# Attention in a six-layer stack: probabilities turned in 32x32 blocks on VectorE, weighed by 32 keys on four row groups, and a new order of work

## The reference

```
q, k, v = split(x @ Wqkv)                 # 3 x 1024 columns
q = l2norm(q) per head;  k = l2norm(k) per head
q = q*cos + rotate_half(q)*sin            # position tables, scaled
k = k*cos' + rotate_half(k)*sin'
for each block of 32 queries: sim = q @ k.T over the 64 keys of its own block and the one before
sim = where(mask, -max, sim);  attn = softmax(sim)
out = attn @ v;  x = out @ Wo             # 1024 -> 128, added to x
x = x + W2 @ (lin * gelu(gate)),  lin, gate = W1 @ layernorm(x)
```

## Time and profile before

| | us |
|---|---|
| median of 3 runs | 3809.59 |
| lowest and highest run | 3805.08, 3809.89 |
| span of the profiled execution | 3803.9 |
| stack0: first projection to last MLP product | 105.9 to 1734.7 |
| mixer | between the stacks |
| stack1: last MLP product | 3797.6 |

### The profile page before, as it was taken

One profiled execution on the slowest core, in us unless ns is written; L12 is line 12 of the kernel. 1 busy time (PEld: TensorE's weight loads), 2 busy tenths in 40 slices (PEclk: granted clock), 3 DMA queues, 4 the chain that ended last, 5 costly groups with the idle time before them and its releaser, 6 DMA issues. The chain is left out here.

```text
span 3803.9 us, 157044 instructions
## 1 busy us (share of the span) xinstructions
PE 3594.4 (94%) x61680; PEld 2336.5 (61%) x61680; DVE 3264.6 (86%) x11515; ACT 2374.7 (62%) x4331; POOL 2752.8 (72%) x2632
## 2 busy tenths in 40 slices
PE   6799999999999999997699689999999999999998
PEld 4466666666666666662466456666666666666665
DVE  6898888888888889865799798889898888889885
ACT  2567667666766767663422257667676766767665
POOL 1788888878888888852144288888887888888883
PEclk9899999999999999998799699999999999999999
DMA  1232323323322332220000132233233232332222
GB/s 46 77 85 71 81 73 78 87 67 74 85 73 69 85 75 66 66 65 16 0 1 6 29 81 72 74 87 78 71 80 76 71 81 74 83 78 68 66 69 57
DMA packets 170286, 250.95 MB, mean 66 GB/s; under 512 B 36544, under 2 KB 67264, under 8 KB 169408
## 3 DMA queue, kind: packets, MB, share of 16 engines
q1 hardware_dynamic: 169536, 240.72, 25.4%
HBM read 38.21 MB, written 1.05 MB: 10 GB/s over the span
## 5 line engine op out<-in xcount | busy, mean ns | idle before, releaser
L592 PE MATMUL stack_work<-stack_w_qkv,stack_xs 128*128 128x512 f32 x2304 | 1148.0, 604 | 34.4 <-ACT stack_sq L883 17.8
L1244 POOL TENSOR_TENSOR stack_roped<-stack_rot_c,stack_rot_s 128x512 f32<-128x512 f32 x768 | 984.6, 1304 | 148.5 <-DVE stack_rot_s L1052 148.2
L1254 POOL TENSOR_TENSOR stack_roped<-stack_roped,stack_rnorm 128x512 f32<-128x512 f32 x768 | 794.6, 1045 | 188.7 <-DVE stack_rnorm L1084 188.7
L883 ACT ACTIVATE stack_sq<-stack_work 128x512 f32<-128x512 f32 x768 | 443.3, 594 | 485.6 <-DVE stack_rot_s L1052 485.1
L1050 DVE TENSOR_TENSOR stack_rot_c<-stack_work,rot_tables 128x512 f32<-128x512 f32 x768 | 526.8, 686 | 130.4 <-PE stack_work L592 112.9
L592 PEld LDWEIGHTS stack_work<-stack_w_qkv,stack_xs 128*128 128x128 f32 x2304 | 400.5, 191 | 384.4 <-issue 323.9
L1270 POOL TENSOR_TENSOR stack_s_m<-stack_s_m,stack_inv 128x512 f32<-128x512 f32 x384 | 400.8, 1044 | 276.4 <-DVE stack_inv L1113 276.1
L1052 DVE TENSOR_TENSOR stack_rot_s<-stack_work,rot_tables 128x512 f32<-128x512 f32 x768 | 521.6, 679 | 0.0
L1061 DVE TENSOR_REDUCE stack_ssq<-stack_sq 128x8 f32<-128x512 f32 x768 | 496.7, 667 | 6.0 <-issue 4.4
L641 PEld LDWEIGHTS stack_bank_o<-stack_p_t,stack_v_w 64*64 64x64 f32 x24576 | 394.5, 135 | 171.9 <-issue 147.4
L600 PE MATMUL stack_work<-ident,stack_roped 128*128 128x128 f32 x3072 | 452.2, 280 | 8.3 <-issue 5.8
(11 more groups left out here) (257 smaller groups left out, 5269.0 us busy)
## 6 DMA issues: line engine op xcount, KB each, us to landing
stack_v_w<-stack_v_nat SPq DMA_DIRECT2D x1152, 128.0 KB
stack_v_w<-stack_v_nat SPq DMA_DIRECT2D x768, 64.0 KB
stack_w_qkv<-table_ffn_qkv SPq DMA_DIRECT2D x192, 96.0 KB, 2.3
stack_w_o<-table_ffn_wo SPq DMA_DIRECT2D x12, 512.0 KB, 4.2
stack_w<-table_ffn_w SPq DMA_DIRECT2D x12, 384.0 KB, 3.3
stack_w<-table_ffn_w SPq DMA_DIRECT2D x12, 192.0 KB, 3.1
x_outer<-L_attn_a_X SPq DMA_DIRECT2D x4, 256.0 KB, 6.9
ret_xpos<-table_xpos SPq DMA_DIRECT2D x1, 1024.0 KB, 6.2
```

What stands on the lines that cost most here:

```text
L592: pe.matmul(bank[:, :], xs[:, T, :], w_qkv[:, g.half, col:col + 512], start=True, stop=True).then_inc(done["proj_" + c], 1)
L883: act.activation(sq[:, i % 2, :], work[(BANK["p_" + c][T] + g.row) % 4][:, :], ACT.Square).then_inc(done["squared_" + c], 1)
L1244: pool.tensor_tensor(roped[:, i, T % 2, :], rot_c[:, i % 2, :], rot_s[:, i % 2, :], ALU.add).then_inc(done["roped_" + c], 1)
L1254: pool.tensor_tensor(r, r, rnorm[:, T % 2, i, :].unsqueeze(2).broadcast_to([P, 8, HD]), ALU.mult).then_inc(done["united_" + c], 1)
```

## The change: what it does

- VectorE turns the probabilities, in 32x32 blocks in SBUF (a new step `turn_probs` on VectorE, two instructions of 128x512 per tile). TensorE's `turn_probs` and ScalarE's `probs_out` go.
- `weigh` is one step with 128 products per tile: 32 rows (keys) each, 64 columns, 32 moving columns, on 4 row groups by 2 column groups. For each block of queries the product with the keys before and that with its own keys are added in PSUM. Each row group writes its own bank. The own keys' values are read in place from `v_nat` (now four tiles deep); only the values 32 positions back are moved, with two transfers per tile in place of ten.
- The four banks `quad` hold the scores (banks 0 and 1) and the weighed heads (all four). `weigh` waits until the masks of the scores before are through, `scores` until `heads_out` has copied the heads. `heads_out` is one copy of 128x1024.
- q is not normed by POOL: its inverse norm is the scale of each mask pass, a value per partition. `unit` is left for k0 and k1 only.
- POOL's `stage` goes; projections read `xst` directly.
- `scores` is one step with all 64 products; it waits for all four chunks.
- All engines get a new order, written out for each T, with other lags (first projection at lag 3, weighing at 8, `project_out` at 9 or 8), a new bank table, and four more slots at the end of a stack.

The core of the diff:

```diff
-        v_nat = sb("v_nat", [P, 2, 2, 8, HD])
-        v_w = sb("v_w", [P, 2, 4, 8, HD])
+        v_nat = sb("v_nat", [P, 4, 2, 8, HD])
+        v_prev = sb("v_prev", [P, 2, 2, 8, HD])
...
-        p_t = sb("p_t", [P, 2, 4, P])
+        p_t = sb("p_t", [P, 2, 2, PAIRS, 2, WINDOW])
...
-        bank_s = [ps("bank_s0"), ps("bank_s1")]
-        bank_o = ctx.enter_context(nc.psum_tensor(shared["tag"] + "bank_o", [P, 2, 512], F32))
+        quad = ctx.enter_context(nc.psum_tensor(shared["tag"] + "quad", [P, 4, 512], F32))
...
-            run_slots(16 * (DEPTH - 1), 4 * (DEPTH - 1), DEPTH - 1, 1, 16 + 12)
+            run_slots(16 * (DEPTH - 1), 4 * (DEPTH - 1), DEPTH - 1, 1, 16 + 16)
...
-                for gp in range(2):
-                    half = 64 * gp
-                    sp.dma_start(v_w[half + 32:half + 64, b, 0, :, :], v_nat[0:32, b, gp, :, :]).then_inc(v_in[b], 16)
-                    sp.dma_start(v_w[half:half + 32, b, 0, :, :], v_nat[96:P, 1 - b, gp, :, :]).then_inc(v_in[b], 16)
-                    for n4 in range(1, 4):
-                        sp.dma_start(v_w[half:half + 64, b, n4, :, :], v_nat[32 * (n4 - 1):32 * (n4 + 1), b, gp, :, :]
-                                     ).then_inc(v_in[b], 16)
+                sp.dma_start(v_prev[WINDOW:P, b, :, :, :], v_nat[0:P - WINDOW, n % 4, :, :, :]).then_inc(v_in[b], 16)
+                sp.dma_start(v_prev[0:WINDOW, b, :, :, :], v_nat[P - WINDOW:P, (n - 1) % 4, :, :, :]).then_inc(v_in[b], 16)
...
-            def weigh(t, T, g, j):
...
-                for half in range(2):
-                    for n in range(4):
-                        for odd in range(2):
-                            for gp in range(2):
-                                m, at = 2 * half + odd, P * half + WINDOW * n
-                                last = pe.matmul(bank_o[HD * odd:HD * (odd + 1), gp, at:at + WINDOW],
-                                                 v_w[64 * gp:64 * gp + 64, T % 2, n, 2 * m + j, :],
-                                                 p_t[64 * gp:64 * gp + 64, j, m, WINDOW * n:WINDOW * (n + 1)],
-                                                 start=True, stop=True)
+            def weigh(t, T, g):
...
+                for j in range(2):
+                    for gp in range(2):
+                        for half in range(2):
+                            at = WINDOW * (4 * j + 2 * gp + half)
+                            for own in range(2):
+                                values = v_nat[:, T, gp, :, :] if own else v_prev[:, T % 2, gp, :, :]
+                                for n in range(4):
+                                    rows = slice(WINDOW * n, WINDOW * (n + 1))
+                                    for odd in range(2):
+                                        m = 2 * half + odd
+                                        last = pe.matmul(quad[HD * odd:HD * (odd + 1), n, at:at + WINDOW],
+                                                         values[rows, 2 * m + j, :], p_t[rows, T % 2, j, 2 * m + gp, own, :],
+                                                         start=not own, stop=bool(own))
+                last.then_inc(done["weighed"], 1)
...
+                act.copy(o_t[:, T % 2, :, :].rearrange("p i (n q) -> p n i q", n=4),
+                         quad[:, :, 0:PAIRS * WINDOW].rearrange("p n (i q) -> p n i q", q=WINDOW)
+                         ).then_inc(done["ot_set"], 1)
...
             def mask_max(t, T, g, j):
...
+                wait(dve, "unit_set", t)
+                apart(dve, t)
                 wait(dve, "scored", t)
-                wait(dve, f"pe_pt{j}", t - 2)
...
-                    last = dve.tensor_tensor_reduce(s_m[:, T % 2, j, hp, :], bank_s[j][:, 64 * hp:64 * hp + 64],
-                                                    mask[:, first:first + 2 * WINDOW], 1.0, LOWEST, ALU.add, ALU.max,
-                                                    smax[:, T % 2, j, hp:hp + 1])
+                    i, h = CHUNKS.index(f"q{hp // 4}"), 2 * (hp % 4) + j
+                    last = dve.tensor_tensor_reduce(s_m[:, T % 2, j, hp, :], quad[:, j, 64 * hp:64 * hp + 64],
+                                                    mask[:, first:first + 2 * WINDOW], rnorm[:, T % 2, i, h:h + 1],
+                                                    LOWEST, ALU.add, ALU.max, smax[:, T % 2, j, hp:hp + 1])
...
+            def turn_probs(t, T, g, j):
+                if not live(t):
+                    return
+                wait(dve, f"prob{j}", t)
+                wait(dve, "weighed", t - 2)
+                dve.transpose(p_t[:, T % 2, j, :, :, :].rearrange("p h f q -> p (h f q)"),
+                              s_m[:, T % 2, j, :, :].rearrange("p h k -> p (h k)")).then_inc(done[f"turned_p{j}"], 1)
```

More of the change, by code:

```diff
@@ L412, in ffn_stack @@
             "xn_nat", "x_turned", "x_back", "pe_back", "x_added"))
[L413 removed]
+        early = [quad[:, n, :] for n in range(4)]
         def natural(s):
@@ L583, in _, with project, turn @@
         def _(pe):
-            def project(t, T, g, c, bank):
+            def project(t, T, g, c):
                 if not live(t):
                     return
[L587 to L590, removed]
+                if c == FIRST_IN and T == 0:
+                    wait_x(pe, g.number - BATCH)
+                    apart(pe, t)
+                    pe.wait_ge(qkv_in, (g.layer + (layer0 + 1)) * 256)
                 col = 512 * PARTS[c]
-                pe.matmul(bank[:, :], xs[:, T, :], w_qkv[:, g.half, col:col + 512], start=True, stop=True
-                          ).then_inc(done["proj_" + c], 1)
-            def turn(t, T, g, c, bank):
+                pe.matmul(work[(BANK["p_" + c][T] + g.row) % 4][:, :], xst[:, g.row, P * T:P * (T + 1)],
+                          w_qkv[:, g.half, col:col + 512], start=True, stop=True).then_inc(done["proj_" + c], 1)
+            def turn(t, T, g, c):
                 if not live(t):
                     return
-                wait(pe, "united_" + c, t)
+                wait(pe, ("roped_" if c[0] == "q" else "united_") + c, t)
+                bank = work[(BANK["t_" + c][T] + g.row) % 4]
                 for n in range(4):
@@ L602, in turn, with scores @@
                 last.then_inc(done["turned_" + c], 1)
-            def scores(t, T, g, part):
+            def scores(t, T, g):
                 if not live(t):
                     return
-                wait(pe, f"kept_k{part}", t)
-                wait(pe, f"kept_q{part}", t)
-                apart(pe, t)
-                for hp in range(4 * part, 4 * part + 4):
+                for c in CHUNKS:
+                    wait(pe, f"kept_{c}", t)
+                    apart(pe, t)
+                for hp in range(PAIRS):
                     for j in range(2):
@@ L645, in weigh @@
-                last.then_inc(done[f"weighed{j}"], 1)
-            def project_out(t, T, g, bank):
-                if not live(t):
-                    return
-                wait(pe, "ot_set0", t)
-                wait(pe, "ot_set1", t)
+                wait(pe, "ot_set", t)
                 if T == 0:
                     pe.wait_ge(wo_in, (g.layer + (layer0 + 1)) * 16)
+                bank = work[(BANK["wo"][T] + g.row) % 4]
                 for n in range(PAIRS):
@@ L661, in center, with variance @@
                 wait(pe, "mid_set", 4 * g.number + 3)
-                pe.matmul(bank[:, :], center_m[:, :], mshift[:, g.pair, 0:SEQ], start=True, stop=True
+                pe.matmul(work[(BANK["ct"] + g.row) % 4][:, :], center_m[:, :], mshift[:, g.pair, 0:SEQ], start=True, stop=True
                           ).then_inc(done["pe_center"], 1)
-            def variance(g, bank):
+            def variance(g):
                 if not live_group(g):
@@ L668, in variance, with up @@
                 wait_group(pe, "center_sq", g)
-                pe.matmul(bank[:, :], mean_m[:, :], c_sq[:, :], start=True, stop=True).then_inc(done["pe_var"], 1)
-            def up(g, kind, k, bank):
+                pe.matmul(work[(BANK["va"] + g.row) % 4][:, :], mean_m[:, :], c_sq[:, :], start=True, stop=True
+                          ).then_inc(done["pe_var"], 1)
+            def up(g, kind, k):
                 if not live_group(g):
@@ L914, in values_out @@
                 wait(act, f"proj_v{gp}", t)
-                if live(t - 1):
-                    act.wait_ge(v_in[(T - 1) % 2], (2 * g.number + (tile0 // 2 + (T - 1) // 2 + 1)) * 160)
-                act.copy(v_nat[:, T % 2, gp, :, :],
+                wait(act, "weighed", t - 3)
+                act.copy(v_nat[:, T, gp, :, :],
                          work[(BANK[f"p_v{gp}"][T] + g.row) % 4][:, :].rearrange("p (h d) -> p h d", d=HD)
@@ L1229, in _ @@
         def _(pool):
-            def stage(t, T, g):
-                if not live(t):
-                    return
-                wait_x(pool, g.number - BATCH)
-                wait(pool, "proj_" + LAST_IN, t - 4)
-                apart(pool, t)
```

(1 more changed line is left out.)

694 lines of the change are left out of this document (394 added, 300 removed).

## The result

The changed kernel takes **4524.07 us** (median of 4 runs, 4511.60 to 4529.44), the kernel before 3807.34 (4 runs, 3804.12 to 3809.89). The ratio is 1.188, 95% interval 1.1861 to 1.1898. The forecast was 3835 and its range ended at 3970. The likeliest case had "slower" as the larger part of its chance, and slower it is, but by 717 us where 25 were forecast, and for a reason that no case had. The profiled execution has a span of 4509.7 us.

What follows compares the result with a forecast made beforehand. TensorE bounded the kernel before; the bound was to move to VectorE, 16.4 plus 0.15 of waits, 16.55 against 16.46 us per tile: +17 over 192 tiles, +12 at the ends, from 3809.6 to 3839, rounded to 3835; range 3680 to 3970.

Steps and rivals of the forecast that it cites:

- The likeliest case: Whole kernel: TensorE relieved by about 1 us, VectorE takes 2 us more and sets the pace; 3790 to 3900, chance 0.40.
- part (3) of TensorE: Weighing: 256 passes of 32 keys at 8.3 ns plus 0.1 for the pause, against 1.84 us now, +0.38 per tile.
- Transposes gone from TensorE (-0.93): TensorE: the eight transposes of the probabilities, two blocks, go; -0.93 us per tile.
- entries (-0.42): TensorE: scores and weighing one block each instead of two, so two fewer tiled blocks to enter and leave; -0.42 us per tile.
- Ends of the stacks (+12): First projection one slot later and last MLP product two: about +6 us per stack, +12.
- VectorE (16.4): VectorE per tile: 14.4 us, plus 1.26 for block transposes and 0.96 for mask-pass scale, less 0.2: 16.4 us.
- Rival C of the prediction: VectorE: a block transpose costs twice a pass, 1.2 us; VectorE 17.5, 4040 us, slower; chance 0.10.
- Rival A: VectorE: mask-pass scale costs nothing, or the norm's steps wait much less; VectorE 15.4, 3678 us, faster; chance 0.34.
- Rival B: TensorE: weighing passes stay at 14.4 ns on eight tiles; TensorE 16.9, slot 17.1, 3945 us, slower; chance 0.16.
- The ring of shared banks: Weighing, copy, scores and masks chained by shared banks set the slot; would need over 16 us, counted about 8; no chance.

Runs made afterwards that it cites:

- own_only: The changed kernel with the products with the keys before left out of weighing, 128 passes instead of 256, so another output; 3848.24 us.
- own_const: own_only with a constant 1.0 as the scale of the mask pass, so the query norm is left out too; 3689.25 us.
- split2: The changed kernel with weighing issued in two parts of 128 passes, other products between them, and slight shifts in order; 4128.56 us.
- scores_burst: The kernel before with the second half of the scores issued four times over, output unchanged; 4718.45 us.
- split4: The changed kernel with weighing issued in four parts of 64 passes and the scores in two parts; 4168.18 us.
- split2_qpool: split2 with a constant in the mask pass and POOL multiplying by the query norm instead; 4046.94 us.
- weigh_twice: The kernel before with every weighing product issued twice, output unchanged; 4181.83 us.

## Why the prediction was wrong

**The step that failed** is part (3) of TensorE, "256 x 8.3 = 2.12 us, plus 0.1". It was mis-sized in two ways. The first is the rate: 8.3 ns came from a stretch of 0.1 us, while the same rows have 64 passes in 0.65 us, 10.2 ns. Weighing runs near that at full clock (x132 in 1.27 us), and at 12.2 ns over the layer, its share of the lower clock included. The second is larger: the sum took for granted that a long burst goes on as a short one begins. It doesn't: 2.04 us per tile of standing still in weighing, 0.34 in the scores, and behind these the lower clock, with about 1.5 us more in the full-size products. With the rate that makes 5.0 us, and TensorE, forecast at 15.3, sets a slot of 20.3. So the bound did not move to VectorE, and that the change is slower, as the forecast had it, was luck: it had VectorE as the reason. Twice the passes, issued as one step, are what put 512 instructions in a row, and the one step I had booked as part of a gain of 0.42.

**Transposes gone from TensorE (-0.93), entries (-0.42).** own_only bears the rest of the sum out in part. With half of weighing's passes off, the forecast sum is 14.2 us a tile; TensorE is busy 15.0. The transposes' 0.93 went whole. Scores and weighing together fell from 3.72 to 2.92, about what fewer and faster passes were to give (0.78). But turns and projections took 0.34 more than before, and nothing of the 0.42 for entries can be seen; no run isolates it.

**Ends of the stacks (+12).** From a stack's first projection to its first scores it takes 32.5 us where it took 23.7, and from the last tile's scores to the last MLP product 53 in both kernels: about +18 for both stacks, where 12 were forecast.

**VectorE (16.4)** was right: 16.3 busy in the changed kernel, 16.5 as a bound in own_only. Behind a block transpose the next instruction starts after 0.627 us (own_only; 0.63 was taken, and the row below has its duration), and the mask passes start 0.205 us apart (0.20). Rival C of the prediction (1.2 us a transpose) is out. The Trainium skill, VectorE: DVE Perf Modes, The three transpose paths, has 311 ns for 128x128 in bf16; grown with the elements, the prediction's estimate of 1.24 us, it is twice the measured time.

```profile
L1121 DVE STREAM_TRANSPOSE stack_p_t<-stack_s_m x384: 656/698/719, 155.7 to 3809.3; 128x512 f32<-128x512 f32 x192
```

**Rival A** fell with own_const. **Rival B** had the right engine and sign and a wrong cause: a pass costs about 10 ns, not 14.4, and its slot of 17.1 was still 3.2 short. **The ring of shared banks** had no chance and deserved none: in the changed layer's waits of TensorE neither the copy of the heads nor the masks appear. The Trainium skill, TensorEngine Tiling, Instruction Overhead, has about 60 cycles for a matmul, by the prediction's estimate 6.4 us for weighing. Pass by pass the trace contradicts it (about 10 ns); the block's 5.2 us came nearer to it than my 2.2, for another reason.

What was left out of the rivals was a limit that the kernel before does not show, because its tiled blocks are short. Its instruction queue was in the page (499 packets, 8.18 MB), and in the layer of the earlier trace rows no wait of TensorE comes from it. One place between 500 and 1500 us does show TensorE standing for issue, where the loop over layers jumps back, with passes at the lower clock behind it:

```profile
835.55 2.74 PE L592 MATMUL stack_work<-stack_w_qkv,stack_xs 128*128 128x512 f32 x4 [3.74 <-issue]
```

The question that would have found the limit: how long do 256 instructions last on this engine, before and after? Before, a layer's 5017 passes, 10034 instructions and more, last 263 us, 6.7 us per 256, and the densest 256 in a row last 3.5 us, with other work between two tiled steps. After, the densest last 1.2. So the kernel before seems to have run just clear of the limit.

Left open: how the clock would have behaved with 32-row tiles and no standstill at all (no run had both in full), what part of the half-clock time is paid by which product, and what sets the start of the next packet. No version here that computes the whole was faster than the kernel before; the best is 4047 us.

## What to carry to other kernels

Count instructions in a row, not only their time. A step of many small tiled products can run through its instructions faster than new ones come (here 512 in a row, 256 of them used up in 1.3 us, where the next 256 came after 3.6), and the same products in two parts with full-size products between them gave 395 of 4524 us back, though not all. Idle time of TensorE put down to "issue" inside a step without waits is the sign to look for, and a lower clock behind it the second bill.

## What the runs showed of the hardware that was not expected

- TensorE can stand still at the edges of blocks of 256 of its own instructions. Where it does, the next block is begun 3.6 us (median; from 2.5) after the one before in the changed kernel, and 5.1 us (3.4 to 9.9) in split2.
- All stretches at 1.2 GHz between 500 and 1500 us, in all nine kernels (the changed one 41, scores_burst 20, split2 18, split4 17, split2_qpool 15, own_only 8, own_const 6, weigh_twice 4, the kernel before 1), begin during or within 5 us of a standstill of over 1 us. A standstill doesn't always bring one: the changed kernel had 61 of over 1 us, and 45 had such a stretch begin in that time.
- A transpose of 128x512 in float32 in 32x32 blocks has nearly the price of the rotations over the same 512 elements: 0.627 us against 0.60, from start to start.
- Tiled passes on eight tiles start every 10 ns or so over 128 of them (x132 in 1.27 us in weighing), for 64-row and 32-row tiles alike, though the first 32 start within 0.27 us.
